# Layers 0 and 1 of a decoder block: scores led by four sequences, sums and maxima turned in other PSUM banks, projections earlier, the output bias in a matmul, stacks in 8 KB rows

## Chip, cores and metric

One NeuronCore of a Trainium2 chip. The metric is the device time of one execution in microseconds (us); less is better. Before: 1677.13 us, median of 3 runs (1676.5 to 1684.85).

## What is computed

Four decoder layers on x of 32 sequences x 128 tokens x 128 features, with a context of the same shape. Each layer adds a gated cross attention and a gated feed-forward part:

```python
x = x + tanh(g_xattn[n]) * xattn_n(layernorm(x), ctx, ctx)   # n = 0..3
x = x + tanh(g_ffn[n]) * ffn_n(layernorm(x))
# xattn of layers 0 and 1: 16 heads of 8
q, k, v = xn @ Wq.T + bq, ctx @ Wk.T + bk, ctx @ Wv.T + bv    # layer 0: rotary turn of q and k
attn = softmax(q @ k.T / sqrt(8), axis=-1)                    # per sequence and head, 128 x 128
out = (attn @ v) @ Wo.T + bo
```

The change touches the attention of layers 0 and 1 alone. The rest of the program (their feed-forward parts and layers 2 and 3) is the same in both kernels.

## The kernel before, in words

`heads_attention` (line 166) is called once for layer 0 (with the rotary turn, `rope`) and once for layer 1. Every engine runs its own hand-written order, joined by semaphores. The 32 sequences j make 8 groups g of 4; a "step" is one pass of the loop over j (lines 449, 558, 646, 748), j counted on all engines, and c = j % 4 is the place of the step in its group, t = j // 4.

**Exact products from bf16.** k and q are in fp32. Each is split into three bf16 parts whose sum is the fp32 value (`split`, line 612, on GpSimd; for group 0 `split_first`, line 693, on VectorE). A head has 8 features, and a score is the sum over the 9 pairs of parts, so a contraction over 9 x 8 = 72 rows. These rows are called the stack: `stack["k"]` holds in its three blocks of 24 rows the k parts, `stack["q"]` the q parts in another order, so that each pair meets once. Rows and heads are rearranged between partitions by way of DRAM: `store` (line 273) writes the parts from SBUF to a scratch tensor, `load` (line 284) reads them back in stack order. The stack of a group has two halves (`hf`) of two sequences, and there are two buffers (g % 2). A load waits until the parts are stored and until the transposed scores of the same half of group g-2 are made (line 288).

In the kernel before k's nine blocks are written out to DRAM in three stores of 384 KB, and loaded by one DMA of 72 rows per half (lines 276 to 292); q is stored once and loaded by three DMAs of 24 rows per half. In the stack tile a row is [head, 512 tokens], so a half of it comes in pieces of 256 bf16, 512 bytes.

**Scores twice.** `scores(j, u)` (line 363) makes q k' of four heads (u = 0..3) in bank 0 or 1; VectorE takes the maxima with a minus sign (`maxima`, line 706); GpSimd splits the 16 maxima per token in three bf16 parts (`split_max`, line 624); TensorE turns them (`turn_max`, line 390), ScalarE copies them to SBUF (`max_out`) and issues a small DMA that puts them in three more rows of q's stack (`max_rows`), against rows of ones in k's. `scoresT(j, u)` (line 377) then makes the transposed scores less the maximum in bank 2 or 3, of which ScalarE takes the exponential (`exps`).

**The rest of a sequence.** `attend` (line 402) multiplies by v and a column of ones into bank 4 (A); ScalarE copies it (`attn_out`); `turn` (line 414) turns it into bank 7 (M); VectorE divides by the sums (`normalise`, line 713); `back` (line 422) turns it back, ScalarE copies (`aT_out`), `out` (line 426) multiplies by Wo, and VectorE adds it to x (`update`, line 723). `turn` writes all of bank M and so waits until the update before it has read its result (`s_x`, line 417). The output bias, with v's bias folded in, times tanh(g), is added to x by GpSimd (`add_bias`, line 605).

**Projections** of group t + 2 lie in group t: x's turn (`turn_xn`) and k at c = 0, q at c = 1, v at c = 2, in banks 5 and 6; bank 6 (`bankP1`) also takes the turned maxima, so that the projections, the turn of x and `turn_max` wait for each other. In layer 0 VectorE rotates k and q (`rotate`, line 680), in layer 1 ScalarE empties them (`evacuate`). LayerNorm: VectorE's statistics (`moments`, line 667), GpSimd's 1/sqrt (line 596), ScalarE's four normalisations in one go (`normalise_x`, line 496).

**The lead.** In step j TensorE makes scoresT(j), scores(j + 3), attend(j - 1), back(j - 2), out(j - 2), turn(j - 1) and turn_max(j + 2), in this order:

```python
                unit(1)
                if 1 <= j <= NSEQ:
                    attend(j - 1)
                if j >= 2:
                    back(j - 2)
...
                unit(2)
                unit(3)
                if j >= 2:
                    out(j - 2)
...
                if 1 <= j <= NSEQ:
                    turn(j - 1)
```

A unit is four transposed scores and four scores (line 453). Before the loop stand the projections of groups 0 and 1 and the scores of the first three sequences.

## Time and profile before

| what | value |
|---|---|
| median of 3 runs | 1677.13 us |
| profiled execution | 1673.37 us, span 1671.6 us |
| granted TensorE clock, mean | 0.894 |
| TensorE busy | 1391.4 us, 83% of the span |
| VectorE, ScalarE, GpSimd busy | 869.9, 553.4, 416.5 us |
| DMA | 151.38 MB, mean 91 GB/s |
| attention of layer 0 | from the start to 264 us |
| attention of layer 1 | from 399 to 632 us |

Busy time of an engine is the union of its instructions; TensorE's ends are modelled, so back-to-back matmuls overlap a little in the rows. "Idle before" is the time in which an engine stood before an instruction, and behind the arrow stands what ended it; "issue" is put where the profile shows no releaser. The granted clock is TensorE's, in parts of 2.4 GHz, and it has two levels, 0.5 and 1.

### The profile page before, as it was taken

The page shows a single profiled execution, that of the slowest core. Times are in us where ns is not written, and L with a number is a line of the kernel's source. Part 1 is how long each engine was busy: PE and PEld are TensorE (multiplying, and loading weights), DVE is VectorE, ACT ScalarE, POOL GpSimd, SP SyncE. Part 2 cuts the span into 40 slices and gives each one's busy share as a digit, 9 for nine tenths or more (in the row PEclk, how much of TensorE's full clock was granted, in tenths as well). Part 3 has the DMA queues.
Part 4 walks back from the last instruction along what each step waited for, and adds up shares of the span by engine and source line. Part 5 has one row for each costly group of instructions (what it writes and reads, how often), then busy time and mean ns, then how long its engine had stood idle before and what let it go on. Part 6 is the DMA issues. An engine that isn't in the chain of part 4 may idle for free. (4 is left out here: it accounts for less than half of the span.)

```text
span 1671.6 us, 26273 instructions
## 1 busy us (share of the span) xinstructions
PE 1391.4 (83%) x8869; PEld 873.1 (52%) x8869; DVE 869.9 (52%) x2507; ACT 553.4 (33%) x1291; POOL 416.5 (25%) x729
## 2 busy tenths in 40 slices
PE   5788885995788885897898599473999999999998
PEld 2566663553566663564787376352444444444443
DVE  4566654885465552333465333574446446446435
ACT  1356554662476651222564133240011011011001
POOL 2666621101665611000244322531000000000000
PEclk8799877997699997999677699795999999999999
DMA  6766660002676727600010111242102202202200
GB/s 162 203 152 151 156 146 1 1 1 61 162 167 164 164 56 319 260 0 15 17 32 20 46 54 46 63 139 102 75 28 107 100 9 107 92 17 107 89 19 13
DMA packets 134175, 151.38 MB, mean 91 GB/s; under 512 B 12150, under 2 KB 117942, under 8 KB 128806
## 3 DMA queue, kind: packets, MB, share of 16 engines
q1 hardware_dynamic: 127494, 142.28, 29.1%
q0 software_dynamic: 3296, 6.76, 1.4%
q8 instruction: 70, 1.15, 0.3%
q10 hardware_dynamic: 3264, 0.79, 0.2%
q14 instruction: 51, 0.42, 0.1%
HBM read 99.33 MB, written 49.48 MB: 89 GB/s over the span
## 5 line engine op out<-in xcount | busy, mean ns | idle before, releaser
L2700 DVE TENSOR_TENSOR l3f_weighted_T<-l3f_w_e,l3f_xnT 128x512 f32<-128x512 f32 x128 | 88.3, 691 | 129.6 <-PE psum L2451 115.3
L2451 PE MATMUL psum<-l3f_weighted_T,w_l3f_q 128*128 128x512 f32 x256 | 133.7, 604 | 16.3 <-DVE l3f_weighted_T L2700 14.5
L2451 PE MATMUL psum<-l3f_weighted_T,w_l3f_k 128*128 128x512 f32 x256 | 131.6, 596 | 0.0
L2451 PE MATMUL psum<-l3f_weighted_T,w_l3f_v 128*128 128x512 f32 x256 | 131.4, 595 | 0.0
L710 DVE TENSOR_REDUCE l1x_minus_max<-psum 128x4 f32<-128x512 f32 x128 | 85.6, 687 | 79.2 <-PE psum L373 78.7
L2460 PE MATMUL psum<-l3f_weighted_T,w_l3f_o 128*128 128x512 f32 x256 | 124.3, 624 | 1.7 <-DVE l3f_weighted_T L2700 1.7
L2700 DVE TENSOR_TENSOR l3f_weighted_T<-l3f_w_e,l3f_oT 128x512 f32<-128x512 f32 x128 | 88.4, 692 | 57.2 <-PE psum L2460 29.6
L710 DVE TENSOR_REDUCE l0x_minus_max<-psum 128x4 f32<-128x512 f32 x128 | 85.5, 687 | 58.8 <-PE psum L373 57.8
L531 ACT ACTIVATE l0x_probsT<-psum 128x512 f32<-128x512 f32 x128 | 73.8, 594 | 56.9 <-PE psum L386 48.6
L111 POOL TENSOR_TENSOR l3f_ln_rstd<-l3f_ln_mean_var,eps 128x4 f32<-128x4 f32 x8 | 1.9, 242 | 355.7 <-DVE l3f_ln_mean_var L104 355.7
L531 ACT ACTIVATE l1x_probsT<-psum 128x512 f32<-128x512 f32 x128 | 73.7, 593 | 34.8 <-PE psum L386 25.6
L2460 PEld LDWEIGHTS psum<-l3f_weighted_T,w_l3f_o 128*128 128x128 f32 x256 | 39.3, 188 | 82.8 <-DVE l3f_weighted_T L2700 78.1
L2451 PEld LDWEIGHTS psum<-l3f_weighted_T,w_l3f_v 128*128 128x128 f32 x256 | 48.9, 191 | 61.8 <-issue 61.8
L2451 PEld LDWEIGHTS psum<-l3f_weighted_T,w_l3f_k 128*128 128x128 f32 x256 | 48.9, 191 | 61.8 <-issue 61.8
L2451 PEld LDWEIGHTS psum<-l3f_weighted_T,w_l3f_q 128*128 128x128 f32 x256 | 44.6, 192 | 60.4 <-issue 44.3
L373 PE MATMUL psum<-l1x_k_stack,l1x_q_stack 72*128 72x128 bf16 x512 | 55.1, 237 | 22.0 <-issue 15.0
L373 PE MATMUL psum<-l0x_k_stack,l0x_q_stack 72*128 72x128 bf16 x512 | 56.1, 240 | 15.0 <-issue 9.4
L386 PE MATMUL psum<-l1x_q_stack,l1x_k_stack 75*128 75x128 bf16 x512 | 51.8, 228 | 2.9 <-DMA l1x_q_stack<-l1x_minus_max_T 2.9
L386 PE MATMUL psum<-l0x_q_stack,l0x_k_stack 75*128 75x128 bf16 x512 | 53.2, 232 | 1.0 <-DMA l0x_q_stack<-l0x_minus_max_T 1.0
L373 PEld LDWEIGHTS psum<-l1x_k_stack,l1x_q_stack 72*128 72x128 bf16 x512 | 37.9, 106 | 26.3 <-issue 23.6
L373 PEld LDWEIGHTS psum<-l0x_k_stack,l0x_q_stack 72*128 72x128 bf16 x512 | 38.5, 108 | 19.8 <-issue 16.5
L2000 DVE TENSOR_TENSOR l_h_tile<-psum,w_l2f_b 128x512 f32<-128x512 f32 x39 | 27.0, 692 | 41.5 <-PE psum L1633 40.3
(486 smaller groups left out, 2988.4 us busy)
## 6 DMA issues: line engine op xcount, KB each, us to landing
l3f_w_e<-l3f_weights_scratch SPq DMA_DIRECT2D x32, 1024.0 KB, 4.7
sorted_x<-zeros SPq DMA_DIRECT2D x1, 16896.0 KB, 59.6
l0x_k_scratch<-l0x_k_parts SPq DMA_DIRECT2D x24, 384.0 KB, 4.1
l0x_k_stack<-l0x_k_scratch SPq DMA_DIRECT2D x16, 576.0 KB
l0x_q_stack<-l0x_q_scratch SPq DMA_DIRECT2D x48, 192.0 KB
l1x_k_scratch<-l1x_k_parts SPq DMA_DIRECT2D x24, 384.0 KB, 4.7
l1x_k_stack<-l1x_k_scratch SPq DMA_DIRECT2D x16, 576.0 KB
l1x_q_stack<-l1x_q_scratch SPq DMA_DIRECT2D x48, 192.0 KB
```

The costliest lines, as they stand in the source:

```text
L111: pool.tensor_tensor(k.rstd[:, :], k.mv[:, :, 1], k.eps[:, :], ALU.add).then_inc(k.s_vare, 1)
L373: ins = pe.matmul(bankS[u % 2][:, seq(i)], stack["q"][0:SROWS, g % 2, h, seq(c)], stack["k"][0:SROWS, g % 2, h, seq(c)], start=True, stop= ...
L386: ins = pe.matmul(bankT[u % 2][:, seq(i)], stack["k"][:, g % 2, h, seq(c)], stack["q"][:, g % 2, h, seq(c)], start=True, stop=True)
L531: act.activation(pT[:, j % 2, 4 * u:4 * u + 4, :], bankT[u % 2].rearrange("p (i q) -> p i q", i=4), ACT.Exp, scale=scale).then_inc(s_exp, 1)
L710: dve.tensor_reduce(nm[:, j % GS, 4 * u:4 * u + 4], bankS[u % 2].rearrange("p (i t) -> p i t", i=4), AX, ALU.max, negate=True).then_inc(s_ ...
L2000: dve.tensor_tensor(hp[:, u % 2, :], bankU[u % 2][:, :], w["l2f_b1"][:, bass.ds(e * HID, HID)], ALU.add)\
L2451: ins = pe.matmul(bank[:, :], w[name][:, e, :], xe[:, e % 2, :], start=(e == 0), stop=(e == NE3 - 1))
L2460: pe.matmul(bankO[g % 2][:, :], w["l3f_o"][:, e, :], xe[:, e % 2, :], start=(e == 0), stop=(e == NE3 - 1))\
L2700: dve.tensor_tensor(xe[:, e % 2, :], wE[:, g % 2, e, :], src, ALU.mult).then_inc(s_xe, 1)
```

## The change

1. `LEAD` is 4: in step j the scores of j + 4 are made.
2. `turn` writes bank A, from which `attn_out` has just copied; `normalise` reads it there and comes at the end of step j - 1's work on VectorE; the next `attend` waits for the product (`s_an`). `back` comes before `attend`.
3. `turn_max(j + 3)` stands at the end of step j and writes a third quarter of bank M. `max_out` and `max_rows` follow it on ScalarE behind the fourth exponential.
4. Projections: k and q of group t + 3 at c = 2 and c = 3, x's turn at c = 3, v of group t + 2 at c = 0; group 2's k and q stand in the prologue. Normalisation by ScalarE is spread over four steps; rstd and shift have two buffers.
5. The bias goes into the output's accumulation group as one bf16 matmul over three rows (the three bf16 parts of the bias, each in a row of its own by a mask); `add_bias` is gone, and eight small VectorE operations on three partitions make the rows.
6. k and q are each stored once per half (q's parts 0 and 1 a second time, so that blocks 0 to 2, 1 to 3 and 2 to 4 are the three rotations) and loaded by three DMAs of 24 rows. Scratch and stack have the half outside, so that a stack row of a half is one run of 16 heads x 256 tokens, 8 KB.

The diff, cut to its core:

```diff
-LEAD = 3
+LEAD = 4
...
+        blocks = {"k": NPART, "q": 2 * NPART - 1}
+        scratch = {n: nc.dram_tensor(f"{name}_{n}_scratch", (2, 2, blocks[n], P, HALF), BF16).ap() for n in "kq"}
+        stack = {n: sb(f"{n}_stack", [TROWS, 2, 2, HEADS, HALF], BF16) for n in "kq"}
...
-        loads = {"k": 1, "q": NPART}
-        stores = {"k": NPART, "q": 1}
+        loads = {"k": NPART, "q": NPART}
+        stores = {"k": 1, "q": 2}
...
+                for hf in range(2):
+                    to = scratch[n][g % 2, hf].rearrange("a p t -> p a t")
+                    sp.dma_start(to[:, 0:NPART, :], parts[n][:, :, half(hf)]).then_inc(s_stored[n][hf], 16)
+                    if n == "q":
+                        sp.dma_start(to[:, NPART:2 * NPART - 1, :], parts["q"][:, 0:NPART - 1, half(hf)])\
+                          .then_inc(s_stored["q"][hf], 16)
...
+                for s in range(NPART):
+                    first = s if n == "q" else 0
+                    sp.dma_start(stack[n][s * block_rows:(s + 1) * block_rows, g % 2, hf, :, :]
+                                 .rearrange("r h t -> r (h t)"), rows_of(scratch[n][g % 2, hf, first:first + NPART]))                      .then_inc(s_stack[n][g % 2][hf], 16)
...
                 store("k", g)
+                store("q", g)
                 load("k", g, 0)
-                store("q", g)
                 load("q", g, 0)
...
-                pe.wait_ge(s_xnT, x_turned)
-                if rope:
-                    pe.wait_ge(s_out["k"], k_out)
-                    pe.wait_ge(s_out["q"], q_out)
-                pe.matmul(bankP1[0:NPART * HEADS, seq(j % GS)], mp[:, j % GS, :], k.ident_bf[:, :],
+                if j >= LEAD + 1:
+                    pe.wait_ge(s_x, j - LEAD)
+                pe.matmul(bankM[0:NPART * HEADS, 2 * P:3 * P], mp[:, j % GS, :], k.ident_bf[:, :],
...
             def attend(j):
...
-                    pe.wait_ge(s_ae, j)
+                    pe.wait_ge(s_an, j)
...
             def turn(j):
                 pe.wait_ge(s_ae, j + 1)
+                for u in range(4):
+                    ins = pe.transpose(bankA[:, seq(u)], ae[:, seq(u)], k.ident[:, :])
+                ins.then_inc(s_turn, 1)
+
+            def back(j):
+                pe.wait_ge(s_an, j + 1)
+                pe.wait_ge(s_mT, min(j + LEAD + 1, NSEQ))
                 if j >= 1:
                     pe.wait_ge(s_x, j)
...
+                pe.matmul(bankM[:, P:2 * P], aT[:, j % 2, :], w["wo"][:, :], start=True, stop=False)
+                if j == 0:
+                    pe.wait_ge(s_bias_rows, 1)
+                pe.matmul(bankM[:, P:2 * P], ones_row[:, 0:P], bias_row[:, 0, :], start=False, stop=True).then_inc(s_o, 1)
...
+            for j in range(LEAD):
                 for u in range(4):
                     scores(j, u)
-                turn_max(j - 1, 2, 2, 2)
+                if j >= 1:
+                    turn_max(j - 1)
+                if j == 1:
+                    project_k(2)
+                if j == 2:
+                    turn_xn(2)
+            project_q(2)
...
                 unit(1)
+                if j >= 2:
+                    back(j - 2)
                 if 1 <= j <= NSEQ:
                     attend(j - 1)
...
                 unit(2)
-                unit(3)
                 if j >= 2:
                     out(j - 2)
...
+                if c == 3 and t + 3 < NG:
+                    turn_xn(t + 3)
+                unit(3)
                 if 1 <= j <= NSEQ:
                     turn(j - 1)
+                if j + LEAD - 1 < NSEQ:
+                    turn_max(j + LEAD - 1)
+                if c == 0 and t + 2 < NG:
+                    project_v(t + 2)
+                if c == 2 and t + 3 < NG:
+                    project_k(t + 3)
+                if c == 3 and t + 3 < NG:
+                    project_q(t + 3)
```

ScalarE, GpSimd and VectorE follow this order. ScalarE's step is exps 0 and 1, aT_out, attn_out, exps 2, (at c = 3 xnT_out), exps 3, max_out, max_rows, then v_out or evacuate, then one quarter of normalise_x. GpSimd's is split_max(j + 3), then q's split at c = 0, moments at c = 2, k's split at c = 3. VectorE's is three maxima, update, the fourth maximum, normalise(j - 1), then at c = 1 moments, at c = 2 and 3 rotate (layer 0).

## Rows read from the trace of the kernel before

**Rows 1.** Busy time by stage: us, busy us of each engine, PEclk, DMA share, GB/s

```profile
77.30:264.30 187.00, 159.63 (x2192) 124.14 (x2190) 112.82 (x255) 107.39 (x236) 97.00 (x186) 0.93 0.60 141
457.00:632.60 175.60, 146.95 (x2172) 117.43 (x2170) 99.47 (x235) 112.17 (x246) 83.19 (x174) 0.94 0.58 132
...
100.00:125.00 25.00, 21.72 (x308) 16.90 (x308) 17.52 (x43) 15.54 (x34) 17.53 (x32) 1.00 0.67 159
...
650.00:690.00 40.00, 34.53 (x160) 22.39 (x161) 13.19 (x65) 10.00 (x20) 2.90 (x5) 0.92 1.02 418
```

**Rows 2.** TensorE's waits in layer 0's loop; layer 1's first row reads the same

```profile
PE psum L419 <- DVE x_sb L727: 8.0, 15, 0.5
PE psum L373 <- issue: 5.8, 4, 3.1
PE psum L399 <- POOL l0x_minus_max_parts L632: 5.2, 7, 2.2
PE psum L424 <- DVE l0x_attn L720: 4.3, 5, 0.9
```

**Rows 3.** TensorE's longest wait in layer 1's loop (us in total, times, longest)

```profile
PE psum L373 <- issue: 15.0, 6, 4.9
```

**Rows 4.** The updates of x (line 727): ns min/median/max, first and last start, us

```profile
L727 DVE SCALAR_TENSOR_TENSOR x_sb<-psum,tanh_g,x_sb x32: 350/351/352, 77.3 to 264.0; 128x128 f32<-128x128 f32 x32
...
L727 DVE SCALAR_TENSOR_TENSOR x_sb<-psum,tanh_g,x_sb x32: 350/351/352, 457.0 to 632.2; 128x128 f32<-128x128 f32 x32
```

**Rows 5.** Timeline of one step of layer 1 without projections: start us, us, instruction

```profile
604.72 0.63 PE L419 MATMUL psum<-constants,l1x_attn_sums_T 128*128 128x128 f32 x4 [0.54 <-DVE x_sb L727]
...
605.18 0.39 PE L386 MATMUL psum<-l1x_q_stack,l1x_k_stack 75*128 75x128 bf16 x4
...
605.38 0.26 DVE L718 RECIPROCAL l1x_rsum<-psum 128x16 f32<-128x16 f32 x1 [0.21 <-PE psum L419]
...
605.68 0.29 DVE L720 TENSOR_TENSOR l1x_attn<-psum,l1x_rsum 128x128 f32<-128x128 f32 x1
...
606.18 1.06 PE L410 MATMUL psum<-l1x_probsT,l1x_v_and_one 128*9 128x128 f32 x32
...
608.50 0.44 PE L428 MATMUL psum<-w_l1x_wo,l1x_aT 128*128 128x128 f32 x2
...
608.98 0.35 DVE L727 SCALAR_TENSOR_TENSOR x_sb<-psum,tanh_g,x_sb 128x128 f32<-128x128 f32 x1
...
609.48 0.63 PE L419 MATMUL psum<-constants,l1x_attn_sums_T 128*128 128x128 f32 x4 [0.54 <-DVE x_sb L727]
```

**Rows 6.** Timeline of layer 0: V's projection, and k's behind the output's

```profile
126.76 1.06 PE L360 MATMUL psum<-w_l0x_projections,ctxT 128*128 128x128 f32 x8
...
138.34 0.44 PE L428 MATMUL psum<-w_l0x_projections,l0x_aT 128*128 128x128 f32 x2
...
138.62 1.88 PE L325 MATMUL psum<-ctxT,w_l0x_projections 128*128 128x512 f32 x4
...
140.34 0.60 PE L419 MATMUL psum<-constants,l0x_attn_sums_T 128*128 128x128 f32 x4
```

**Rows 7.** Timeline of layer 1: x's turn, and scores behind a late stack

```profile
509.99 0.66 PE L347 MATMUL psum<-constants,l1x_xn 128*128 128x128 f32 x4 [0.49 <-ACT l1x_xn L501]
...
519.57 0.38 PE L373 MATMUL psum<-l1x_k_stack,l1x_q_stack 72*128 72x128 bf16 x4 [4.25 <-issue]
```

**Rows 8.** DMA issues: out<-in, issuer, count, KB each

```profile
l0x_k_stack<-l0x_k_scratch SPq DMA_DIRECT2D x16, 576.0 KB
```

**Rows 9.** Timeline of the prologues: layer 0's first scores, both first transposed scores

```profile
38.84 1.01 PE L373 MATMUL psum<-l0x_k_stack,l0x_q_stack 72*128 72x128 bf16 x8 [4.57 <-DMA l0x_q_stack<-l0x_q_scratch]
...
51.94 0.58 PE L386 MATMUL psum<-l0x_q_stack,l0x_k_stack 75*128 75x128 bf16 x4 [0.96 <-DMA l0x_q_stack<-l0x_minus_max_T]
...
438.79 0.58 PE L386 MATMUL psum<-l1x_q_stack,l1x_k_stack 75*128 75x128 bf16 x4 [1.68 <-DMA l1x_q_stack<-l1x_minus_max_T]
```

More of the change, by code:

```diff
@@ L372, in scores @@
                     h = 4 * u + i
-                    ins = pe.matmul(bankS[u % 2][:, seq(i)], stack["q"][0:SROWS, g % 2, h, seq(c)],
-                                    stack["k"][0:SROWS, g % 2, h, seq(c)], start=True, stop=True)
+                    ins = pe.matmul(bankS[u % 2][:, seq(i)], stack["q"][0:SROWS, g % 2, c // 2, h, of_seq(c)],
+                                    stack["k"][0:SROWS, g % 2, c // 2, h, of_seq(c)], start=True, stop=True)
                 ins.then_inc(s_S, 1)
@@ L548, in _ @@
                 evacuate("k", g)
-                normalise_x(g)
+                for c in range(GS):
+                    normalise_x(g, c)
                 xnT_out(g)
@@ L635, in _ @@
             pool.wait_ge(s_fill, 4)
[L636 removed]
+            for g in range(3):
                 moments(g)
             split("k", 1)
+            split("q", 1)
             split_max(0)
[L640 removed]
             split_max(1)
[L642 to L644 removed]
+            moments(3)
+            split_max(2)
+            split("k", 2)
             for j in range(NSEQ):
                 t, c = divmod(j, GS)
[L648 to L656 removed]
+                if j + LEAD - 1 < NSEQ:
+                    split_max(j + LEAD - 1)
+                if c == 0 and t + 2 < NG:
+                    split("q", t + 2)
+                if c == 2 and t + 4 < NG:
+                    moments(t + 4)
                 if c == 3 and t + 3 < NG:
[L658 removed]
+                    split("k", t + 3)
         @block.vector
@@ L736, in _ @@
             dve.wait_ge(s_bp, 1)
-            dve.tensor_tensor(bias[:, :], bankM[:, 0:P], w["bo"][:, :], ALU.add).then_inc(s_bias, 1)
-            dve.wait_ge(s_bias, 1)
-            dve.tensor_scalar(gb[:, :], bias[:, :], k.tanh_g[:, gain:gain + 1], None, ALU.mult).then_inc(s_bias, 1)
+            step = Chain(dve, s_bias, 0, 0)
+            part = lambda i: bias_part[:, i, :]
+            pick = lambda i: k.ident[0:NPART, i:i + 1]
+            step(dve.tensor_tensor(bias[:, :], bankM[0:NPART, 0:P], w["bo"][0:NPART, :], ALU.add))
+            step(dve.tensor_copy(part(0), bias[:, :]))
+            step(dve.tensor_tensor(bias_rest[:, :], bias[:, :], part(0), ALU.subtract))
+            step(dve.tensor_copy(part(1), bias_rest[:, :]))
+            step(dve.tensor_tensor(part(2), bias_rest[:, :], part(1), ALU.subtract))
+            step(dve.tensor_scalar(bias_row[:, 1, :], part(0), pick(0), None, ALU.mult))
+            step(dve.scalar_tensor_tensor(bias_row[:, 2, :], part(1), pick(1), bias_row[:, 1, :], ALU.mult, ALU.add))
+            dve.scalar_tensor_tensor(bias_row[:, 0, :], part(2), pick(2), bias_row[:, 2, :], ALU.mult, ALU.add)\
+               .then_inc(s_bias_rows, 1)
             rotate("k", 1)
+            moments(2)
             rotate("q", 1)
@@ L758, in _ @@
                     maxima(j + LEAD, 3)
-                if t + 2 < NG and c == 0:
-                    rotate("k", t + 2)
-                if t + 2 < NG and c == 1:
-                    rotate("q", t + 2)
-                if t + 3 < NG and c == 1:
-                    moments(t + 3)
+                if 1 <= j <= NSEQ:
+                    normalise(j - 1)
+                if c == 1 and t + 4 < NG:
+                    moments(t + 4)
+                if c == 2 and t + 3 < NG:
+                    rotate("k", t + 3)
+                if c == 3 and t + 3 < NG:
+                    rotate("q", t + 3)
 def layer0_attention(nc, k):
```

229 lines of the change are left out of this document (87 added, 142 removed).

## Prediction

> **What bounds the kernel now.** I read the stages first. Of the 1671.6 us of the span, the attention loops of layers 0 and 1 (from the first to the last update of x) take 187 and 175.6 us; TensorE is busy 159.6 and 147.0 of them, VectorE 112.8 and 99.5, and the granted clock is 0.93 and 0.94 [rows 1]. TensorE is the engine with the most work, and it isn't dense. The waits of TensorE say where: in layer 0 the turn of the sums waits 8.0 us for the update of x, the turned maxima 5.2 us for GpSimd, the turn back 4.3 us for the normalised attention, and the scores 5.8 us for "issue" [rows 2]; in layer 1 "issue" is 15.0 us [rows 3] and the update again 8.0. The "issue" waits stand before the scores of a group's first sequence, where the only unmet condition in the code is the landing of the stacks (line 366). The updates' first and last starts give the loops' lengths: 264.0 - 77.3 = 186.7 us and 632.2 - 457.0 = 175.2 us for 31 steps each [rows 4].
>
> One step of layer 1 without projections shows the dense order [rows 5]: turn at 604.72, scores from 605.18, attend at 606.18, output projection at 608.50; then nothing until the update (608.98) is written and the next turn starts at 609.48. So 3.78 us of 4.76 are dense; the output projection's own slot is 0.28 (138.34 to 138.62 [rows 6]), and 0.70 is the wait that the shared bank M makes. A projection of layer 0 takes 1.72 us (138.62 to 140.34), V's 1.06 less the 0.17 by which a modelled end overlaps the next start, 0.89 [rows 6]; layer 1 has one matmul of the two, 0.86; x's turn 0.66 less 0.17, 0.50 [rows 7]. One late stack costs far more: at 519.57 the scores have stood 4.25 us [rows 7], and the clock of such stretches falls from 1.00 to the lower level for a while, which is how layer 1's mean gets to 0.94.
>
> **The change, part by part, TensorE first.** (a) Sums turned in bank A: the turn no longer waits for the update. Dense step: 3.78 + 0.28 = 4.06; the bias matmul (3 rows, bf16, 128 columns) has no row: below by nothing, above by the 0.28 of the fp32 pair; one bf16 matmul of the scores has a slot of 0.06 (16 from 605.18 to 606.18 [rows 5]), nearest in kind, so 0.06, and 0.10 for one more switch between bf16 and fp32. Step: 4.22.
>
> (b) What could stand in that place is now the chain turn, reciprocal, product, turn back, as bank A and the order need the product before the next turn back and attend. In [rows 5] the reciprocal starts 0.66 after the turn, the product ends 0.59 after that. In the new step (start at its first scores) the turn is at 3.70; VectorE takes the fourth maximum at about 3.83 to 4.50 (its pass is 0.69), reciprocal and product until 5.09; the turn back wants it at 4.22 + 1.00 = 5.22. It fits by 0.1 us where no projection separates the steps, by 0.9 or more elsewhere. I cost it at nothing; if it doesn't fit, rival 2.
>
> (c) Maxima turned at the step's end, and scores a step earlier: GpSimd splits (1.2 us) while TensorE works 4 us; the 5.2 us of waits go. The copy and the DMA issue on ScalarE (0.27 + 0.73) now lie between the fourth exponential and the next first one: it starts about 1.2 us into the step and is wanted at 2.23 by the third bank of transposed scores. Queued behind them are only exponentials that wait for TensorE anyway; nothing on the path.
>
> (d) Projections moved up, normalisation in quarters of 0.41 us (durations here and in (c), (e) without a row are medians of their lines): the same TensorE work, without the waits for x (five per layer). LayerNorm statistics on VectorE (1.35 us) after a group's second step delay two maxima: about 0.55 us in three groups, 1.65; and 0.2 for V's copy in five groups, 1.0.
>
> (e) No bias addition on GpSimd (1.27 us per group, hidden before as well): nothing. Its eight small VectorE operations in the prologue lie while TensorE projects: nothing.
>
> (f) Stacks. Rows become 8 KB instead of 512 B. A half of k and q together is 1.18 MB, as before (a load of k is 576 KB [rows 8], q's three together the same); stores fall from 1.57 to 1.05 MB per group but in 512-byte pieces instead of 1 KB, so their time stays. While the queues are full the loads run at 159 GB/s with share 0.67, and the long rows of the zero fill at 418 GB/s with 1.02 [rows 1]: 7.4 or 2.8 us for a half. I take 4.5, nearer the long rows. SP issues 12 loads and 6 stores per group instead of 8 and 4: by at most 0.79 each, 14 us of a 20 us group, without blocking. The lead of four leaves two steps between a half's release (the last transposed scores of its second sequence) and its next use, where three were. First half: q's parts are ready early in a group's second step, stored about 2 us into the third, landed by the fourth; wanted at the next group's first step: about 3 us to spare. Second half: released 3.6 us into the fourth step, landed 7 to 8 us later; wanted 11.4 (layer 1) or 12.2 us later. So the 5.8 and 15.0 us go, and the half clock after them.
>
> **The sum** of a loop, update to update: 25 steps with scores at 4.22, 105.5; four without scores, 3.3 of TensorE and 0.25 of the chain of (b), 3.55 each, 14.2; the last two, 6.4; V, five times 0.89, and five groups of k, q and x's turn: layer 0 5 x (3.44 + 0.50) + 4.45 = 24.15, layer 1 5 x (1.72 + 0.50) + 4.45 = 15.55; (d) 2.65. Layer 0: 152.9 against 186.7, less 33.8. Layer 1: 144.3 against 175.2, less 30.9.
>
> **Prologues.** The first scores start at 38.84 after a wait for q's stack, the loop at 51.94, and its first update comes at 77.3, 25 us later, as the next stacks are late and the clock is low [rows 4, 9]; in layer 1 438.79 and 457.0. With the change the loop starts later, after a fourth sequence and the projections of group 2: GpSimd's chain of two splits (5.7 us each with the rotary sum), three splits of maxima and moments gives about 56 us, layer 1 437.5. But then nothing is missing: two steps (5.1, 4.2 and, in layer 0, 1.8 of GpSimd's lateness) and 3.4 to the update: 70.6 and 450.3. Less 6.7 each. Ends: nothing, as all that TensorE does is the same; 11, if the wait for q's stack (4.57) goes too.
>
> Sum: 33.8 + 30.9 + 13.4 = 78. The profiled execution took 1673.4 us (span 1671.6), 3.8 under the median of the three runs, 1677.1: 1595 beside the first, 1599 beside the median.
>
> **Rivals.**
> 1. *The second halves are still late.* At today's 159 GB/s a half takes 7.4 us, and with 2 us of latency and the next group's store before it the landing is at 11.5 to 12 us: past layer 1's 11.4, and near layer 0's. For: the loads are of 24 rows, three per tensor, and these rows show no such load with long rows. Against: the fill's 418 GB/s. Price: 1.5 us and about 2 us of half clock, in ten groups of two layers taken at six: 20 us, 1619. The Trainium skill (SBUF — State Buffer, "Door 1: The DMA port swizzle") says that partitions p and p + 32 share a port: 64 of the 72 rows then have 8 of 16 ports, 4.7 us a half as an estimate by its port rate, and the sum stays. No run here shows it.
> 2. *The chain in (b) doesn't fit*, since its margin is 0.1 us and VectorE also rotates k and q: 0.3 us more in 50 steps, 15 us, 1614.
> 3. *Slower.* The lead of four keeps a half of each buffer only two steps, and if loads of 24 rows are served by few DMA engines, transfers become the bound. A group of layer 0 lasts 25 us; loads of 2.36 MB and about 5 us of stores fill that at 118 GB/s. Below that rate the change loses; at 60 GB/s a group takes 44 us, 19 more in 14 groups: 1940. For: nothing in the rows; against: the same number of rows per load now gives 159.
> 4. *Only the stack waits go* (5.8 + 15.0 and some 15 of low clock), because each wait removed on TensorE returns at the next engine: 36 us, 1641.
>
> **Chances.** Forecast 0.50; rival 1 0.17; rival 2 0.17; rival 4 0.11; rival 3 0.05. The likeliest has 1585 to 1610 (prologue ends, +-0.2 us a step); rivals 1 and 2 together reach 1635, and 4 is at 1641. Range 1580 to 1642: what is left out is rival 3 and a part of the extremes. A measurement of this kernel tells about 0.5% (8 us) from no change: only rival 3 is above; faster 0.93, same 0.02, slower 0.05.
>
> **What would show it.** Right: the turn follows the scores without a wait for the update (L419's 8.0 us gone); steps of 4.2 to 4.3 us between updates in layer 1's stretches without projections; the granted clock 0.98 or more in both loops; GB/s over DMA share well above 240. Wrong: TensorE waiting for the stacks before a group's third sequence (rival 1); turn back or attend waiting for the product (rival 2); DMA share near 0.75 throughout with loads in flight longer than 11 us (rival 3); new waits of ScalarE's first exponential on the maxima's copy and issue (c).

## Result: 1625.0 us, 3.4% less, and the profile after

The changed kernel takes 1625.03 us (median of 4 runs, 1612.68 to 1634.38); the kernel before, run beside it, 1679.95 us. The ratio is 0.966, with a 95% interval of 0.960 to 0.972. The forecast was 1599 us with a range of 1580 to 1642: the sign and the range hold, but the gain is 55 us instead of 78. The profiled execution took 1634.4 us, span 1632.6, 39 us less than the span before.

Busy time by stage, first update of x to last (us, busy us of PE, weight loads, DVE, ACT, POOL, granted clock, DMA share, GB/s), the kernel after; it answers to [rows 1]. Third and fourth row: layer 1 up to its last group, and the stretch behind that group's late stack:

```profile
73.50:239.70 166.20, 157.25 (x2206) 119.17 (x2202) 107.26 (x243) 105.23 (x233) 84.71 (x168) 0.97 0.61 138
438.40:596.20 157.80, 153.20 (x2185) 118.64 (x2182) 94.67 (x223) 109.07 (x243) 71.95 (x158) 0.94 0.52 123
...
440.00:547.00 107.00, 106.78 (x1608) 84.22 (x1607) 73.01 (x171) 81.42 (x183) 66.95 (x135) 1.00 0.70 166
549.76:568.00 18.24, 18.24 (x187) 14.15 (x191) 8.71 (x16) 7.34 (x16) 1.76 (x8) 0.50 0.25 51
```

TensorE is now dense: 106.8 of 107 us in the third row, at full clock. Its busy time is much as before (157.3 and 153.2 us against 159.6 and 147.0); what went is idle time. The fourth row is where layer 1 still loses: TensorE is as dense there, but at a clock of 0.50, for 18 us.

The updates of x in the kernel after, layer 0 and layer 1 [rows 4]:

```profile
L719 DVE SCALAR_TENSOR_TENSOR x_sb<-psum,tanh_g,x_sb x32: 340/343/352, 73.5 to 239.5; 128x128 f32<-128x128 f32 x32
L719 DVE SCALAR_TENSOR_TENSOR x_sb<-psum,tanh_g,x_sb x32: 340/343/352, 438.4 to 596.0; 128x128 f32<-128x128 f32 x32
```

TensorE's waits in the kernel after, in layer 0's loop, then layer 1's prologue, then layer 1's loop [rows 2, 3]:

```profile
PE psum L362 <- issue: 3.1, 1, 3.1
PE psum L375 <- issue: 1.7, 1, 1.7
PE psum L414 <- DVE l0x_attn L712: 1.4, 2, 0.7
PE psum L388 <- POOL l0x_minus_max_parts L627: 1.1, 4, 0.3
...
PE psum L375 <- DMA l1x_q_stack<-l1x_minus_max_T: 4.6, 1, 4.6
PE psum L362 <- issue: 3.8, 1, 3.8
...
PE psum L362 <- issue: 1.7, 1, 1.7
```

The waits for the update, 8.0 us in either loop, are gone; the turn back waits 1.4 us for the product, in two places behind the last scores; the maxima wait 1.1 us for GpSimd instead of 5.2. Three waits for stacks remain (scores are line 362 now): 3.1 and 1.7 us before the first sequence of the last group of each layer, and 3.8 us in layer 1's prologue. One wait is for a DMA of maxima, 4.6 us. The 1.7 us of line 375 in layer 0 come back under "Left open".

One step of layer 1 without projections in the kernel after [rows 5]:

```profile
538.37 0.60 PE L406 MATMUL psum<-constants,l1x_attn_sums_T 128*128 128x128 f32 x4
...
539.18 0.25 DVE L710 RECIPROCAL l1x_rsum<-psum 128x16 f32<-128x16 f32 x1
...
539.46 0.29 DVE L712 TENSOR_TENSOR l1x_attn<-psum,l1x_rsum 128x128 f32<-128x128 f32 x1
...
539.98 0.28 PE L414 MATMUL psum<-constants,l1x_attn 128*128 128x128 f32 x1
...
541.64 0.46 PE L418 MATMUL psum<-w_l1x_wo,l1x_aT 128*128 128x128 f32 x2
542.04 0.23 PE L421 MATMUL psum<-l1x_out_bias_rows,l1x_ones_row 3*128 3x128 bf16 x1
542.20 0.40 PE L375 MATMUL psum<-l1x_q_stack,l1x_k_stack 75*128 75x128 bf16 x4
```

The turn starts without any wait. The product ends at 539.75, 0.23 us before the turn back: the chain of (b) fits. Output projection and bias take 542.20 - 541.64 = 0.56 us of TensorE, where 0.28 + 0.06 + 0.10 = 0.44 was forecast.

The profiled execution is 39 us over the forecast (span 1632.6 against 1593.5, the sum of the forecast's column). Where they lie (us; all from first and last updates and spans, as above; the last column is a variant that comes below, version 2, in which only the placement of the stack rows differs):

| stretch | before | forecast | after | rows by three |
|---|---|---|---|---|
| start to first update, layer 0 | 77.3 | 70.6 | 73.5 | 71.4 |
| loop of layer 0 | 186.7 | 152.9 | 166.0 | 157.3 |
| from there to layer 1's first update | 193.0 | 186.3 | 198.9 | 192.4 |
| loop of layer 1 | 175.2 | 144.3 | 157.6 | 146.9 |
| rest | 1039.4 | 1039.4 | 1036.6 | 1039.4 |

Both loops and the way to layer 1's first update fell short, the last even longer than before. The question for the experiments: is it the transfers (rival 1), the slots on TensorE, or both; and which of the six parts of the change carries the gain.

What the transfers look like in the kernel after, in layer 1's prologue: loads by SyncE (SPq, three at a time), the DMAs of the maxima by ScalarE (ACTq), and the first things that TensorE lacks:

```profile
405.07 1.37 SPq L295 DMA_DIRECT2D l1x_k_stack<-l1x_k_scratch  x3
...
407.71 1.18 SPq L295 DMA_DIRECT2D l1x_k_stack<-l1x_k_scratch  x3
...
408.94 1.18 SPq L295 DMA_DIRECT2D l1x_q_stack<-l1x_q_scratch  x3
409.55 0.73 ACTq L518 DMA_DIRECT2D l1x_q_stack<-l1x_minus_max_T  x1
...
419.17 0.59 PE L362 MATMUL psum<-l1x_k_stack,l1x_q_stack 72*128 72x128 bf16 x4 [3.83 <-issue]
...
429.15 0.61 PE L375 MATMUL psum<-l1x_q_stack,l1x_k_stack 75*128 75x128 bf16 x4 [4.60 <-DMA l1x_q_stack<-l1x_minus_max_T]
```

Three loads (576 KB) take 3.85 us from first to last packet (median over k's loads, worked out from the records of the queue; 4.8 us for q's, which overlap k's): about 153 GB/s. Before, k's 576 KB came in one DMA of 72 rows with 512-byte packets, and at the same rate (3.87 us, median of the 14 that lie alone in the queue). The 12 KB of maxima issued at 409.55 landed at 427.85, with the last packets of the loads issued before it, both halves of k and q (428.25). The median time for maxima to land is 4.3 us in the kernel after and 3.3 before, the longest 18.3 and 8.2.

### The profile page after: what moved, and what is told of

Its sections match the earlier page's. It is cut to its first block and busy times, and to the rows that moved or that the text cites. A ratio compares the mean times of both kernels' runs of the same rounds, so it can differ in the third digit from the quotient of the medians.

```text
span 1632.6 us, 26439 instructions
## 1 busy us (share of the span) xinstructions
PE 1399.9 (86%) x8933; PEld 868.7 (53%) x8933; DVE 869.3 (53%) x2519; ACT 551.7 (34%) x1291; POOL 396.9 (24%) x713
## 5 line engine op out<-in xcount | busy, mean ns | idle before, releaser
L2455 PE MATMUL psum<-l3f_weighted_T,w_l3f_q 128*128 128x512 f32 x256 | 133.7, 604 | 15.9 <-DVE l3f_weighted_T L2704 14.1
L375 PEld LDWEIGHTS psum<-l1x_q_stack,l1x_k_stack 75*128 75x128 bf16 x512 | 34.8, 103 | 23.3 <-issue 9.9
L1637 PE MATMUL psum<-w_l2f_w,l_xT_tile 128*128 x78 | 45.4, 669 | 0.9 <-ACT l_xT_tile L1767 0.5
```

The costliest lines, as they stand in the source:

```text
L375: ins = pe.matmul(bankT[u % 2][:, seq(i)], stack["k"][:, g % 2, c // 2, h, of_seq(c)], stack["q"][:, g % 2, c // 2, h, of_seq(c)], start=T ...
L1637: pe.matmul(bankU[u % 2][:, :], xT[:, u % NXT, :], w["l2f_w1"][:, bass.ds(e * HID, HID)], start=True, stop=True).then_inc(s_up, 1)
L2455: ins = pe.matmul(bank[:, :], w[name][:, e, :], xe[:, e % 2, :], start=(e == 0), stop=(e == NE3 - 1))
```

## Experiments

Twelve kernels. Each time is a median, and each ratio is to runs of the kernel before made beside it (medians 1683.1 to 1688.7 us). The kernel before itself moves between these rounds and the one of the result (1680.0 us), so a difference of medians across rounds is good to some 5 us only. "By three" means rows of a load on every third partition, as in version 2.

**1. Loads written in 512-byte pieces** (after).

```diff
-rows_of = lambda ap: ap.rearrange("a (d h) t -> (a d) (h t)", h=HEADS)
+rows_of = lambda ap: ap.rearrange("a (d h) t -> (a d) h t", h=HEADS)
```

> The changed kernel, with every stack load cut back into runs of one head (512 bytes) instead of rows of 8 KB; order, stores and layout in DRAM stay. Theory A (a load of 24 rows is bound by where its rows lie, and not by the length of a run; the changed kernel's own trace shows 3.6 to 3.9 us for three loads of 192 KB, 151 to 164 GB/s, what the kernel before had with 512-byte runs): the three loads still take 3.6 to 4.0 us, the small DMAs of the maxima land sooner than the 6 to 7 us that they need behind 8 KB packets (about 4), the prologue's wait for them in layer 1 (4.6 us) shrinks, and the time is the changed kernel's within 10 us, more likely below it (1615 to 1628). Rival B (long rows are what paid): loads slow down to 5 us or more for three, stacks come late in every group, time 1640 to 1660.

1633.35 us, ratio 0.966 (0.960 to 0.973). The edit did nothing to the transfers: the profile counts the same packets, DMA queue 1 moves 2304 packets of 8192 bytes per layer in both, as head and token are one run in scratch and stack anyway. So this says nothing of long against short rows, and neither theory was tested. It serves as a second sample of the kernel after: a profiled span of 1640.1 against 1632.6, layer 0's loop 176.3 against 166.0, layer 1's first update 5.7 us sooner after the start of its attention. Ten us in one stage of one profile are what late stacks do by chance here. Packets, kernel after, then this one:

```profile
DMA packets 74722, 143.03 MB, mean 88 GB/s; under 512 B 13431, under 2 KB 53879, under 8 KB 64743
```

```profile
DMA packets 74722, 143.03 MB, mean 87 GB/s; under 512 B 13431, under 2 KB 53879, under 8 KB 64743
```

**2. Rows of a load on every third partition** (after). Row r of block s goes to partition 3 r + s instead of 24 s + r, in both stacks alike; the products are the same.

```diff
-stack[n][s * block_rows:(s + 1) * block_rows, g % 2, hf, :, :]
+stack[n][s:SROWS:NPART, g % 2, hf, :, :]
```

> The changed kernel, but the 24 rows of a load go to every third partition of the stack (s, s + 3, ... s + 69) instead of 24 neighbours, for k and q alike, so that the same pairs of parts meet. Theory A (neighbouring partitions share a way into SBUF, so that 24 of them are served at about 160 GB/s): three loads take 2.7 to 3.0 us instead of 3.6 to 3.9 (200 GB/s or more), the DMA share falls, the late stacks before the last group's scores (3.1 us in layer 0, 1.7 in layer 1) and their stretches of half clock go, the prologue shortens by 2 to 4 us a layer: 1600 to 1612. Rival B (12 DMA engines with two rows each are the bound, or DRAM is): three loads still take 3.6 to 3.9 us and the time is the changed kernel's within noise (1615 to 1630).

1609.41 us, ratio 0.954 (0.948 to 0.959), 16 us less than the kernel after, and 24 less than version 1, which moves the same packets as the kernel after and was run beside this one. Its stages:

```profile
71.40:229.00 157.60, 152.78 (x2207) 116.19 (x2205) 107.20 (x242) 104.92 (x233) 84.20 (x166) 1.00 0.51 146
421.10:568.30 147.20, 144.14 (x2186) 112.52 (x2183) 94.08 (x223) 108.37 (x243) 71.77 (x158) 1.00 0.47 133
```

The same bytes pass with a DMA share of 0.51 and 0.47 instead of 0.61 and 0.52, no wait for a stack in the loops is over 0.5 us, and the clock is 1.00. An 8 KB packet takes 0.46 us on average instead of 0.62 (a quarter of them 0.32 or less, against one in twenty), and k's 576 KB 3.34 us instead of 3.85, a smaller step than the 2.7 to 3.0 expected. The transfers were too slow, as rival 1 of the prediction has it, and the placement of the rows is a cause. Two other readings, the number of DMAs and the time of their issue, are taken up in versions 6 and 11. The loops are within 4.4 and 2.6 us of the forecast.

**3. Bias added by GpSimd again** (after; no bias matmul, `add_bias` behind the maxima of a group's third step).

```diff
-pe.matmul(bankM[:, P:2 * P], aT[:, j % 2, :], w["wo"][:, :], start=True, stop=False)
-pe.matmul(bankM[:, P:2 * P], ones_row[:, 0:P], bias_row[:, 0, :], start=False, stop=True).then_inc(s_o, 1)
+pe.matmul(bankM[:, P:2 * P], aT[:, j % 2, :], w["wo"][:, :], start=True, stop=True).then_inc(s_o, 1)
...
+                if c == 2 and t + 2 < NG:
+                    add_bias(t + 2)
```

> The changed kernel with the output bias added to x by GpSimd as before (1.27 us per group), and the output projection a single fp32 matmul group. Theory C (TensorE is dense in the steps, so its instructions are the time): the bias matmul's slot of 0.16 us and about 0.09 of the slot before it (0.37 against 0.28) go in each of 64 steps, at most 16 us; GpSimd has room. I expect 8 to 14 us less than the changed kernel: 1610 to 1617. Rival D (the steps are bound by a chain through ScalarE or VectorE): no difference, within 3 us.

1619.01 us, ratio 0.960 (0.954 to 0.965): 6 us less than after and 14 less than version 1, which was run beside it, where 8 to 14 were expected; by the intervals it is not apart from either. Steps of layer 1 are 5.0, 5.4, 5.0, 4.4 us instead of 5.3, 5.7, 5.3, 4.5, so one small bf16 matmul between fp32 and bf16 work costs 0.25 to 0.3 us, not 0.16. The last groups' stacks are still late (one step of 10 to 11 us in each layer), and in layer 0 so are three stacks before them (by 1.7 to 2.1 us).

**4. Sums turned in bank A, alone** (before).

```diff
-pe.transpose(bankM[:, seq(u)], ae[:, seq(u)], k.ident[:, :])
+pe.transpose(bankA[:, seq(u)], ae[:, seq(u)], k.ident[:, :])
...
-pe.wait_ge(s_ae, j)   # attend
+pe.wait_ge(s_an, j)
```

> The kernel before with one part of the change alone: the sums are turned in bank A, the turn back waits for the update instead, and attend for the product. Forecast's term (a): the turn's waits for the update (8.0 us in 15 places in each layer, about 0.7 us each with the latency) go and nothing takes their place before the next matmuls: 0.7 us in about 11 of 32 steps per layer, so 12 to 20 us less than the kernel before: 1660 to 1668. Rival (attend now waits for the product, and it comes after a late normalise): no gain, 1675 to 1682.

1683.5 us, ratio 1.001 (0.998 to 1.005): the 12 to 20 us that I expected did not come, and the rival is right. The wait for the update is gone, and in its place `attend` waits for the product. TensorE's first wait in layer 0's loop:

```profile
PE psum L410 <- DVE l0x_attn L720: 14.1, 16, 2.0
```

Bank A alone is worth nothing in the old order. In the kernel after, where the turn back stands before attend and the product is made earlier, the waits for it are 1.4 us.

**5. Both: rows by three and bias by GpSimd** (after).

> The kernel after with both edits: rows of a load on every third partition, and the bias added by GpSimd instead of by a matmul. Theory: the two savings lie on different resources and add. The rows by three gave 1609.4 us, the bias matmul's absence 0.25 to 0.3 us a step in some 50 steps, 13 us where no stall takes it back: 1595 to 1600, loops 144 to 150 (layer 0) and 134 to 138 us (layer 1), last group's stack in time. Rival: with steps shorter by 0.3 us the last stacks come late again (as with the bias edit alone: one step of 10 to 11 us and half clock behind it in each layer): 1605 to 1610.

1596.29 us, ratio 0.947 (0.944 to 0.950), the fastest. With the rows by three the bias edit is worth 13 us, where it was 6 or 14 with neighbouring rows, so the two savings add, within what the runs can tell. Loops of 154.3 and 139.0 us, the first longer than the 144 to 150 expected. Layer 0 gains less because GpSimd now makes the maxima late there (5.4 us of waits, fourth steps 5.3 instead of 4.7).

**6. One load of 72 rows instead of three of 24** (after).

```diff
-for s in range(NPART):
-    sp.dma_start(stack[n][s * block_rows:(s + 1) * block_rows, ...], rows_of(...first:first + NPART]))
+sp.dma_start(stack[n][0:SROWS, g % 2, hf, :, :].rearrange("r h t -> r (h t)"), src)
```

Here `src` gives, for each of 24 rows, the three blocks one behind the other (k's the same block three times).

> The kernel after with each half of k or of q loaded by one DMA of 72 rows (the three block rows of a row one behind the other) instead of three DMAs of 24. Theory P: the rate goes by the groups of partitions that are written at the same time; a DMA that walks 72 neighbouring partitions in order touches few at any time, so 576 KB still take 3.5 us or more (160 GB/s or less), stacks are late as in the kernel after, 1620 to 1640. Rival Q: what counts is how many partitions one DMA spans, or the issue time on SyncE (2.25 us for three loads with rows by three, one DMA here): 576 KB in 2.2 to 2.9 us, no late stack, 1600 to 1610.

1608.93 us, ratio 0.953 (0.950 to 0.957), the same as version 2. k's 576 KB pass in 3.25 us against 3.34 there and 3.85 in the kernel after (medians), packets 0.48 us. Theory P falls in the form it had: neighbouring partitions in one DMA are no harm, as long as it spans 72 of them. But rival Q is only half right, since k's time is above its 2.2 to 2.9 us and the gain is the same with three issues or one. Issue time is not the limit: SyncE issues these 72 rows in 0.77 us, less than three loads of 24 neighbours (0.36 each), and the packets are still the faster ones. Set beside the kernel before, where k's load was one DMA of 72 rows too but in 512-byte packets and took 3.87 us, this one shows that 8 KB rows did bring k something. The kernel after lost it by cutting the load into 24 neighbours. (The source in DRAM differs as well, three copies there and one here, which wasn't tried alone.)

**7. The new stacks alone, neighbouring rows** (before, with part 6 of the change).

> The kernel before with part 6 alone as the kernel after has it (8 KB rows, 24 neighbouring rows a load). With rows by three this gave 1655.0 us (ratio 0.980). Theory: loads are no faster than before (8 KB packets of 0.6 us, 13 GB/s per DMA engine), only the stores are smaller: 1670 to 1684, so that the 28 us of the version by three come from the placement of the rows. Rival: smaller stores and the fewer DMAs before the first scores are the gain: 1655 to 1662.

1689.4 us, ratio 1.005 (1.001 to 1.008): not faster, and slower than the 1670 to 1684 expected. Prologue and loops part ways: layer 0's first update comes at 67.7 us, 9.6 sooner, but the loops take 196.6 and 188.7 us. TensorE's waits in layer 1, prologue included:

```profile
PE psum L382 <- DMA l1x_q_stack<-l1x_minus_max_T: 20.0, 5, 6.0
PE psum L343 <- ACT l1x_xn L497: 12.0, 8, 4.3
PE psum L369 <- issue: 8.9, 4, 4.0
```

The first was 1.7 us in the kernel before's prologue [rows 9]. In the old order SyncE has both halves of a group to load at once, 2.3 MB, and the small DMAs of the maxima land only behind them: four of these waits, of 2.2 to 6.0 us, lie in the loop, before sequences 10, 13, 18 and 21, whose maxima took 9 to 13 us to land. The burst alone doesn't do it: in version 8, the same with rows by three, the longest is 5.8 us.

**8. The same with rows by three** (before).

> The kernel before with only the new scratch and stack (8 KB rows, k stored once per half, q's two stores, three loads each), rows on every third partition; order, banks, lead of three, bias on GpSimd as before. Theory: of the gain, the stacks' waits with the half clock behind them are one part that stands by itself: 5.8 + 15.0 us of issue waits and some 15 us of low clock go, so 1683 - 36 = 1647, steps of layer 1 without 11 to 12 us ones, and the update waits (8.0 us per loop) stay. Rival: with three sequences of lead the stack has a step more, so it was never the transfer that was late but q's parts from GpSimd; then 1670 or more.

1655.04 us, ratio 0.980 (0.976 to 0.985). That is 34 us less than the kernel before beside it, where the theory had 36 (the profiled executions, 1671.6 and 1652.9 us in span, show 19 of them), but not where it had them. First and last updates:

```profile
L724 DVE SCALAR_TENSOR_TENSOR x_sb<-psum,tanh_g,x_sb x32: 349/351/352, 67.9 to 254.9; 128x128 f32<-128x128 f32 x32
L724 DVE SCALAR_TENSOR_TENSOR x_sb<-psum,tanh_g,x_sb x32: 349/351/352, 443.7 to 614.1; 128x128 f32<-128x128 f32 x32
```

Layer 0's loop is 187.0 us, as before (186.7), and layer 1's 170.4 against 175.2; nearly all else comes ahead of the loops. In layer 0's loop the waits for stacks fell from 5.8 to 0.9 us, those for GpSimd's maxima rose from 5.2 to 9.1, those for the update and the product stayed (8.0 and 4.3), and the granted clock is 0.91 instead of 0.93. This is in part what rival 4's reason said (each wait returns at the next engine), in a loop of the old order.

**9. Rows by three and bank A** (before).

> The kernel before with the new stacks by three and the sums turned in bank A, nothing else (attend still stands before the turn back). Theory: bank A alone gained nothing (ratio 1.0014) because attend then waits for the normalised product instead (14.1 us in layer 0) and because stacks came later by as much; with stacks in time only the first reason is left, so 0 to 8 us below the version without bank A: 1640 to 1647 if that one is at 1647. Rival: late stacks alone had hidden it, and the whole 16 us of update waits go: 1631.

1649.39 us, ratio 0.978 (0.973 to 0.982): 6 us under version 8, not apart by the intervals, with attend waiting 13.0 us for the product in layer 0 (14.1 in version 4). The theory holds, the rival (1631) does not.

**10. The old stacks in the new order** (after, part 6 undone).

> The kernel after with scratch, stack, stores and loads of the kernel before (part 6 undone: 512-byte runs, three stores of k, one load of k over 72 rows, one store of q), all else as after. Theory: the loop's gain comes from the order, banks and projections (the kernel before with the new stacks alone kept loops of 187 and 170 us), so most of it stays: 1630 to 1645, with late stacks in some groups, as a lead of four leaves the loads less time. Rival: with the old transfers the lead of four makes them late in most groups: 1660 to 1690, and then the new stacks are what the lead of four rests on.

1672.9 us, ratio 0.993 (0.990 to 0.995). The rival is right, my theory (1630 to 1645) wrong: without part 6 the other five bring 10 us of the 55. Stages and TensorE's first wait in each layer:

```profile
80.80:259.40 178.60, 160.68 (x2206) 121.18 (x2203) 107.57 (x243) 106.03 (x233) 84.74 (x168) 0.93 0.63 146
456.00:641.30 185.30, 162.35 (x2186) 124.89 (x2183) 95.26 (x223) 110.57 (x243) 72.00 (x158) 0.88 0.56 124
```

```profile
PE psum L366 <- issue: 21.1, 7, 7.1
...
PE psum L366 <- issue: 23.4, 7, 5.0
```

The steps in which nothing is late are the same as in the kernel after; what undoes them is one slow step of a group, of 10.7 to 13.6 us in five of layer 1's groups and two of layer 0's. A lead of four leaves the loads a step less, and the old way (three stores of k, and one flag for all of a group's parts) doesn't fit in it; which piece of the old way is too slow wasn't tried.

**11. Every second partition and neighbours in one kernel** (after).

```diff
-stack[n][s * block_rows:(s + 1) * block_rows, ...]
+stack[n][slice(s, 2 * block_rows, 2) if s < 2 else slice(2 * block_rows, SROWS), ...]
```

> The kernel after with two of the three loads of each k and q half on every second partition (0, 2 .. 46 and 1, 3 .. 47) and the third on 48 to 71 in a row: both placements in one kernel. If the rate goes by how many groups of four partitions a load touches (6 for 24 neighbours, 12 for every second, 18 for every third), packets of the first two loads take clearly less than those of the third (about 0.6 us for 8 KB), near 0.31 to 0.45; time between, 1608 to 1620. The Trainium skill (SBUF - State Buffer, Door 1: The DMA port swizzle) says that four neighbours share a port and p and p + 32 do too: then the first two loads reach 8 ports and the third 6, a ratio of 1.33 only, by estimate from its port rule. Rival: placement does nothing, and rows by three only helped because SyncE issues each such load in 0.75 instead of 0.4 us, so that fewer loads are in flight: all packets alike, and 1608 if these loads' issue is slow too.

1611.98 us, ratio 0.957 (0.954 to 0.961), as expected, and not apart from version 2 by the intervals. An 8 KB packet takes 0.54 us on average, between 0.62 (neighbours) and 0.46 (by three). The late stack of layer 0 lies between, too: TensorE waits 2.4 us for it here, 3.1 in the kernel after and 0.5 by three. SyncE issues the spread loads in 0.70 to 0.73 us, against 0.36 (neighbours) and 0.70 (by three). Which packet belongs to which load can't be read where loads overlap, so the two placements can't be compared inside this kernel. The issue time is nearly that of the version by three and yet the packets are slower, which speaks for the placement, as version 6 does; the queue's time tells the same. Queue 1 as a share of 16 engines' span: after, this version, by three:

```profile
q1 hardware_dynamic: 68038, 133.89, 28.0%
```

```profile
q1 hardware_dynamic: 68038, 133.89, 26.8%
```

```profile
q1 hardware_dynamic: 68038, 133.89, 25.3%
```

**12. Version 5 with the bias a step earlier on GpSimd.**

```diff
-if c == 2 and t + 2 < NG:
+if c == 1 and t + 2 < NG:
     add_bias(t + 2)
```

> The kernel after with rows by three and the bias on GpSimd, as in the run that gave 1596.3 us, with one line moved: the addition for group t + 2 stands on GpSimd behind the maxima of a group's second step instead of its third. Theory: in layer 0 the addition made the split of the next maxima late (TensorE waited 5.4 us for GpSimd's parts, fourth steps of 5.2 to 5.3 us instead of 4.4 to 4.8); at its new place it does not, fourth steps fall to 4.5 and layer 0's loop from 154.3 to about 150: 1592. Rival: GpSimd is still in the split of q there, which then ends later and with it the store and the load of q's stack; the wait only moves: 1596, or a late stack, 1600.

1601.29 us, ratio 0.951 (0.949 to 0.954), against 0.947 (0.944 to 0.950) for version 5: no gain, where 1592 us was expected. Fourth steps of layer 0 stay at 5.3 us and the waits for GpSimd at 5.5 us (5.4 in version 5): the place of the addition is not what sets them. That it is the sum of GpSimd's work in a group was not tried.

## Why the forecast was right, and where it was off

The direction and its mechanism were right: TensorE was made dense, and the loops became shorter by idle time. Of the signs that I had named, the update waits are gone and free steps take 4.3 us; but the granted clock is 0.97 and 0.94 instead of 0.98 or more, and GB/s over DMA share is 226 and 237, not well above 240. The size was off by a third (55 us instead of 78), and the term that failed is (f). Point by point:

**(a) Bank A.** Right in the new order: the turn never waits for the update. Off in one term: output and bias take 0.56 us (0.53 with both at their shortest) instead of 0.44, so a free step takes 4.3 instead of 4.22. The nearest row in kind (0.06 for a bf16 matmul among its like) and 0.10 for the switch were too low together; version 3 puts the matmul and its switches at 0.25 to 0.3 us a step, the upper end that I had named (0.28).

**(b) The chain to the product.** Right, with 0.23 us to spare where 0.1 was forecast. Rival 2 did not come. Version 4 shows its price where the order isn't changed: 14.1 us.

**(c) Maxima at the step's end.** Right for GpSimd (1.1 us of waits). What I left out is the DMA behind them: with loads in flight it landed up to 18.3 us after its issue. In layer 1's prologue that is the 4.6 us wait.

**(d) Projections moved up.** Right: groups of 22.8 and 20.8 us, of 22.46 and 20.75 by the forecast's terms (4 x 4.22, the projections, 0.75 for VectorE's part). What the free steps cost more is nearly lost in it.

**(e) Bias off GpSimd.** Nothing gained in layer 1, as said. In layer 0 it was not quite nothing: version 5 with it on GpSimd has 5.4 us of waits there. Still, the matmul costs TensorE more than the addition costs GpSimd: 13 us between versions 2 and 5.

**(f) The stacks.** This is the step that failed. "I take 4.5, nearer the long rows": a half takes 7.9 us in the median of the 32 (6.9 to 13.0), below even the lower of the two rates that I chose between. With 24 neighbouring rows a load, the long packets brought no rate: before, the trace had 512-byte packets of 0.04 us, after 8 KB packets of 0.6 us, about 13 GB/s in both. The fill's 418 GB/s, that I leaned on, was of zeros read from all 128 partitions; a load here writes 24. Version 2 changes nothing but the partitions that a load writes, and the mean packet goes from 13 to 18 GB/s, a half from 7.9 to 6.5 us.

Rival 1 has the rate right but not the place. It makes the second halves late, with a wait before a group's third sequence as its sign. No such wait came. Both waits for stacks in the loops stand before the first sequence of the last group, whose first half I had given "about 3 us to spare". In layer 1 the loads of the first half are issued at 538.38 and 540.34, and those of the second only at 546.99:

```profile
538.38 1.51 SPq L295 DMA_DIRECT2D l1x_k_stack<-l1x_k_scratch  x3
540.34 1.19 SPq L295 DMA_DIRECT2D l1x_q_stack<-l1x_q_scratch  x3
546.99 1.70 SPq L295 DMA_DIRECT2D l1x_k_stack<-l1x_k_scratch  x3
549.76 0.59 PE L362 MATMUL psum<-l1x_k_stack,l1x_q_stack 72*128 72x128 bf16 x4 [1.69 <-issue]
```

The first half's last packet ends at 548.71, 9.4 us after its first. For layer 1's groups g = 2 to 6 there were 2.9 to 3.7 us between the last packet and the scores, so the spare time held where I had looked. But the last of the steps before group g = 7 hold no projections of k and q; so the four pass in 18.3 us instead of 20.8, which I had overlooked. The half clock behind the wait also lasted longer than I had priced it: in layer 1 one wait of 1.7 us, then three steps of 8.3, 7.6 and 7.6 us instead of 4.3, 10.6 us in all. In layer 0 it was 4.1 us (9.0 against 4.9). One late half in each loop is fewer than the six in all that rival 1 counted; but one costs 4 to 11 us and not 3.5. The two errors nearly cancel, so it is in part luck that rival 1's 1619 us is nearer the 1625 measured than the forecast's 1599.

The Trainium skill (SBUF — State Buffer, "Door 1: The DMA port swizzle") offers a reason, and I had it in the prediction and used it on the wrong unit. By its rule four neighbouring partitions share a port, and p and p + 32 do. I took the 72 rows of a stack together: 8 ports, 4.7 us (the sum gives 4.8). But the rows are loaded 24 at a time, and 24 neighbours are 6 ports; at the page's 27.2 GB/s a port, as an estimate, that is 163 GB/s. The trace agrees: 153 with neighbours. Every second partition reaches 8 ports by the rule, every third 10, and packets fall in that order (0.62, 0.54, 0.46 us). The size doesn't agree: ten ports would give 272 GB/s by the same estimate, and k's loads by three pass at 177. So the rule orders the three placements, and what limits the faster ones is open. No run here isolates the clause on p and p + 32.

**Prologues.** Forecast -6.7 each; measured -3.8 in layer 0, and in layer 1 +5.9 from the last update of layer 0. With rows by three they are -5.9 and -0.6. So the placement of the rows cost 2.1 and 6.5 us of it. Of the rest, the forecast took layer 1's first two steps at full clock, and in version 2, where nothing waits long, that stretch has a clock of 0.70:

```profile
405.70:421.10 15.40, 13.94 (x176) 11.81 (x175) 8.79 (x22) 11.26 (x22) 9.25 (x20) 0.70 0.57 158
```

**The sum of the misses.** Of the 39 us, the placement of the rows (after minus by three, loops and prologues) is 2.1 + 8.7 + 6.5 + 10.7 = 28.0 in the profiles, and 16 us by the medians (24 beside version 1). The profiled execution of after is the slowest of its four, and 4.4 of the 8.7 us are the two slow steps of "Left open", which are not shown to come from the transfers. The rest of the program was 2.8 us shorter. The other 13.9 us are the bias's slot (some 50 steps of 0.1 us), layer 1's cold prologue, and steps that were sized a little short.

**Which part carries the gain.** No part does by itself: stacks alone 1.005, order, banks and bias alone (version 10) 0.993, together 0.966. The order makes TensorE dense when nothing is late, but takes a step from the loads; the stacks give it back, but in the old order their loads, on neighbouring rows, come in one burst that blocks the maxima. Version 8 against 2 says the same with fast loads: 0.980 in the old order, 0.954 in the new one.

**Left open.** In layer 0 the kernel after has one wait of 1.71 us at 114.90, between the first and second matmul of a unit of transposed scores, where the code has no wait, and two slow steps behind it (7.1 and 7.3 us instead of 5.2 and 4.8), with the clock at 0.50 for 6.8 us from 115.88. A packet of the instruction queue was in flight from 111.45 for 1.8 us; that it is the cause wasn't tried. Of part 6, the share of k's single store against that of a flag for each half wasn't tried either.

## To carry to other kernels

Ask of each DMA by itself, not of the tile that it helps to fill, which partitions it writes: 24 rows on every third partition cost nothing to arrange and gave 16 us over 24 neighbours, while packets 16 times longer gave those neighbours no rate. A change that shortens the step and one that shortens the transfers may each show no gain alone; before dropping one, test it with the other in place. Small DMAs on the path (here 12 KB of maxima) need the large ones to be spread out, not merely to be early. And count the time to spare in the shortest steps of a loop, here those in which the projections have run out.

## What the runs showed of the hardware

- A DMA of 12 KB from ScalarE's queue landed 18.3 us after its issue, together with the 2.3 MB that SyncE had issued around it, though it was on another queue; alone it takes 1.6 us. The Trainium skill (DMA: Bandwidth & Descriptors, "Back-pressure in remote DMA") says that stalled writes stall an engine's other queues too; it says so of transfers between cores. These runs show the same look within one core, not that it is this mechanism. With rows by three the longest was 5.5 us (5.8 in the old order), with the old 512-byte packets 8.2 (before) and 6.7 (version 10). More than 10 us appear only where 8 KB packets go to 24 neighbours: the kernel after and versions 1, 3 and 7 (13.2, 13.3 and 15.4).
- SyncE takes 0.36 us to issue a load of 24 rows of 8 KB on neighbouring partitions and 0.70 to 0.73 us for the same load on every second or third partition. It was hidden here.
- A wait of TensorE of 1.7 us, behind 107 us of dense work at a granted clock of 1.00 (2.4 GHz), was followed by 18 us at 0.50 (1.2 GHz) in which TensorE was busy all the time: the wait cost 1.7 us, what came behind it about 9. Layer 0's wait of 3.1 us was followed by only 3.4 us at 0.50 (201.22 to 204.63), so the length of a wait doesn't tell its price; no run here shows what does.
